# First expert's low weights on VectorE, and shorter slot ranks, at the head of the two capacity-limited expert stages

## The chip, the cores and the metric

One core of one Trainium2 chip. The metric is the device time of one execution in microseconds (us), the median of three runs.

## The reference, cut to what matters

The program is a chain of twelve residual stages on 2048 tokens of 128 features. Stages 0 and 2 are the same mixture of experts, `_L0_ffn_ref`: tokens fall into 8 groups of 256, each token chooses two of 8 experts, and each expert takes at most C = 64 tokens of a group. First choices are counted first, and the rank of a second choice starts behind them.

```python
m1 = one_hot(argmax(softmax(logits)));  m2 = one_hot(argmax(rest))
p1 = cumsum(m1, axis=-2) - m1
m1 = m1 * (p1 < C)
m1_count = sum(m1, axis=-2)
p2 = cumsum(m2, axis=-2) - m2 + m1_count[:, None, :]
m2 = m2 * (p2 < C)
dispatch = (combine != 0)               # one-hot of the slot p1 or p2, per expert
expert_inputs = einsum('GSEC,GSM->EGCM', dispatch, x)
hidden = gelu(expert_inputs @ w0) * (expert_inputs @ w1)
out = einsum('EGCM,GSEC->GSM', hidden @ wo, combine)
```

## The kernel before

Every stage has a program for each engine (TensorE, ScalarE, VectorE, GpSimd, and SyncE, which issues the loads), written out by hand; the engines meet at a barrier before each stage and otherwise by semaphores. `q.wait_ge(*signal.at(key))` is a wait of one engine for a tick of another; on one engine everything behind such a wait stands still. `chain(a)` on VectorE makes each operation wait for the one before it.

`l0_ffn` is the stage concerned; it runs twice, as stage 0 and stage 2. float32 products are made of three passes with float32r operands, `mm3` (lines 94 to 97): high times high, high times low, low times high. So each operand is split into a high part (a cast) and a low part (the difference).

The head of the stage, from the barrier to the first expert product, goes like this.

- SyncE issues the loads of the weights of experts 0, 1 and 2 at once (lines 844 to 847).
- VectorE finds first and second choices (`first_largest`, lines 673 to 680), as masks `m1b` and `m2b`, which TensorE awaits as `mask_set` 1 and 2.
- TensorE makes ranks by products with a triangular matrix `tri` and a matrix of ones `onesb`: first choices into bank 3 (lines 462, 463), the count of first choices per group and expert into bank 4 (465, 466), second choices into bank 5 (468, 469).
- VectorE turns them into slots (lines 688 to 698). A slot is rank plus one, and zero where the token isn't sent. Lines 689 and 696 zero what lies past the capacity, 692 clamps the counts at 64, 694 adds them to the ranks of the second choices.
- VectorE compares slots with 1 to 64 (`iota`), one operation for each of 16 tiles of tokens, 128 x 512 each (line 703): the one-hots `d[t]`.
- TensorE multiplies the features, high and low (z = 0, 1), by the one-hots (line 479, four products for each of 8 groups g), into six banks in turn; ScalarE copies each bank into `xd` (line 610, 16 copies).
- Meanwhile ScalarE has cast the weights of expert 0 (`split_in(0, k)`, line 596), and GpSimd has made their low parts (line 789, k = 0 with 752 columns and k = 1 with 640), ticking `w_lo`.
- The first expert product, `up(0, 0)`, waits for `xd_set` of group 7 and for the low weights (lines 487 to 492). Its first instruction is the one of line 95.

Behind the one-hots VectorE makes the gates `G` (lines 708 to 711), which TensorE needs after `up(0, 1)`, and then it takes part in the experts: `product` (line 717) and `low` (line 722). GpSimd's next work after line 789 is `high(0, 0)` (line 804), behind the first product. The weights of the other seven experts are split by ScalarE and GpSimd within the experts' loop.

```python
for i in range(8):
    high(i, 0)
    high(i, 1)
    if i + 1 < 8:
        split_in(i + 1, 0)
```

Of the kernel before, what the change touches and what calls it, by code (L numbers as in the profile page):

```python
# [7 lines left out]
ALU = mybir.AluOpType  # L8
ACT = mybir.ActivationFunctionType
F32 = mybir.dt.float32  # L10
# [89 lines left out]
def build(nc, ins, out):  # L100
    ctx = ExitStack()
    with ctx:
        signals = []

        def signal(name):
            signals.append(Signal(ctx.enter_context(nc.semaphore(name))))
            return signals[-1]
# [3 lines left out]
        bank = [wide[i // 2][:, i % 2 * 512:i % 2 * 512 + 512] for i in range(8)]  # L111
# [19 lines left out]
        def take(name, n, dt=F32):  # L131
            size = -(-n * (2 if dt == BF16 else 4) // 64) * 64
            a = nc.sbuf_base
            for lo, hi in sorted(mem["used"]):
                if a < hi and a + size > lo:
                    a = hi
            assert a + size <= nc.sbuf_top, (name, n, a + size, nc.sbuf_top)
            mem["n"] += 1
            mem["used"].append((a, a + size))
            return nc.alloc_sbuf_tensor_at(f"{name}{mem['n']}", [128, n], dt, offset=a)[:, :]  # L140
# [17 lines left out]
        def cB(name):  # L158
            a, b = CB_AT[name]
            return cb[:, a:b]  # L160

        ident, iota = cF("ident"), cF("iota")
        identb, tri, onesb = cB("ident"), cB("tri"), cB("ones")
# [10 lines left out]
        step, steppool = signal("dve_step"), signal("pool_step")  # L174
# [6 lines left out]
        w_hi, w_set, w_lo, x_hi, x_set, x_lo = (signal(n) for n in ("w_hi", "w_set", "w_lo", "x_hi", "x_set", "x_lo"))  # L181
        mask_set, rank, slot_set, one_hot, dispatched = (signal(n) for n in ("mask_set", "rank", "slot_set", "one_hot", "dispatched"))
# [233 lines left out]
        def l0_ffn(n, pre, prepare):  # L416
# [4 lines left out]
            w_in = [[twin("w", size) for size in (FH + 64, 640)] for _ in range(3)]  # L421
            wh = [[take("wh", size, F32R) for size in (FH + 64, 640)] for _ in range(2)]
# [4 lines left out]
            passing = mem["used"][first:]  # L427
            ex, tmp, diff, rest, q1, pos = (te3(take(s, 128)) for s in ("ex", "tmp", "diff", "rest", "q1_", "pos"))
            mx, vm = take("mx", 16), take("vm", 16)
            cnt = take("cnt", 64).rearrange("p (g e) -> p g e", e=8)  # L430
            m1b, m2b = take("m1b", 128, BF16), take("m2b", 128, BF16)
            G = take("G", 512).rearrange("p (t n) -> p t n", t=NT)
            gs = take("gs", 32).rearrange("p (g k) -> p g k", k=4)
# [9 lines left out]
            m4 = lambda z: z.rearrange("p (g j e) -> p g j e", j=2, e=8)  # L443
# [14 lines left out]
            def pe(q):  # L458
                e = q.e
# [2 lines left out]
                e.matmul(bank[3][:, 0:128], tri, m1b, start=True, stop=False, skip_group_check=True)  # L462
                e.matmul(m4(bank[3][:, 0:128])[:, :, 1, :], onesb, m4(m1b)[:, :, 0, :], start=False, stop=True,
                         skip_group_check=True).then_inc(*rank.tick(n, 1))
                e.matmul(bank[4][:, 0:64], onesb, m4(m1b)[:, :, 0, :], start=True, stop=False)
                e.matmul(bank[4][:, 0:64], onesb, m4(m1b)[:, :, 1, :], start=False, stop=True).then_inc(*rank.tick(n, "count"))
                q.wait_ge(*mask_set.at(n, 2))
                e.matmul(bank[5][:, 0:128], tri, m2b, start=True, stop=False, skip_group_check=True)
                e.matmul(m4(bank[5][:, 0:128])[:, :, 1, :], onesb, m4(m2b)[:, :, 0, :], start=False, stop=True,
                         skip_group_check=True).then_inc(*rank.tick(n, 2))  # L470
                q.wait_ge(*x_lo.at(n, 3))
# [10 lines left out]
                def up(i, f):  # L482
                    f0, fn = L0T[f]
                    p0, p1 = up_bank(i, f)
                    s = slice(f0, f0 + fn)
                    xe = [xd[:, i, z, :] for z in range(2)]
                    q.wait_ge(*w_hi.at(n, i, 1))
                    q.wait_ge(*w_lo.at(n, i, 1))
                    if 6 * i + f >= 3:
                        q.wait_ge(*mul_set.at(n, *before(i, f)))  # L490
                    else:
                        q.wait_ge(*xd_set.at(n, 7))
                    if f < 5:
                        mm3(e, p0, [wh[i % 2][0][:, s], w_in[i % 3][0][1][:, s]], xe)
                        a = mm3(e, p1, [wh[i % 2][1][:, s], w_in[i % 3][1][1][:, s]], xe)
                    else:
                        a = mm3(e, p0[0:112, :], [wh[i % 2][0][:, 640:752], w_in[i % 3][0][1][:, 640:752]], xe)
                    a.then_inc(*up_done.tick(n, i, f))
# [166 lines left out]
            def dve(q):  # L665
                e = q.e
                t3 = lambda p: p[:, 0:128].rearrange("p (t e) -> p t e", e=8)

                def chain(a):
                    a.then_inc(*step.tick())  # L670
                    q.wait_ge(*step.now())

                def first_largest(v, mask, number, *shifted):
# [9 lines left out]
                m1, m2 = te3(m1b), te3(m2b)  # L683
# [2 lines left out]
                chain(e.scalar_tensor_tensor(rest, m1, 0.5, ex, ALU.is_lt, ALU.mult))  # L686
                first_largest(rest, m2, 2)
                q.wait_ge(*rank.at(n, 1))
                chain(e.scalar_tensor_tensor(tmp, t3(bank[3]), 64.0, m1, ALU.is_lt, ALU.mult))
                chain(e.scalar_tensor_tensor(q1, t3(bank[3]), 1.0, tmp, ALU.add, ALU.mult))  # L690
                q.wait_ge(*rank.at(n, "count"))
                chain(e.tensor_scalar(cnt, bank[4][:, 0:64].rearrange("p (g e) -> p g e", e=8), 64.0, None, ALU.min))
                q.wait_ge(*rank.at(n, 2))
                chain(e.tensor_tensor(rest.rearrange("p (g j) e -> p g j e", j=2), m4(bank[5][:, 0:128]),
                                      cnt.unsqueeze(2).to_broadcast([128, 8, 2, 8]), ALU.add))
                chain(e.scalar_tensor_tensor(tmp, rest, 64.0, m2, ALU.is_lt, ALU.mult))
                chain(e.scalar_tensor_tensor(tmp, rest, 1.0, tmp, ALU.add, ALU.mult))
                e.tensor_tensor(pos, q1, tmp, ALU.add).then_inc(*slot_set.tick(n))

                def one(t):  # L700
                    q.wait_ge(*slot_set.at(n))
                    q.wait_ge(*x_lo.at(n, 3))
                    e.tensor_tensor(d[t].rearrange("p (e c) -> p e c", e=8), iota[:, 1:65].unsqueeze(1).to_broadcast([128, 8, 64]),
                                    pos[:, t, :].unsqueeze(2).to_broadcast([128, 8, 64]), ALU.is_equal).then_inc(*one_hot.tick(n, t))

                for t in range(NT):
                    one(t)
                chain(e.tensor_reduce(mx, ex, X, ALU.add))
                chain(e.reciprocal(mx, mx))
                q.wait_ge(*w_lo.at(n, "pad"))  # L710
# [72 lines left out]
            def pool(q):  # L783
                e = q.e

                def split_in(i, k):
                    w, low = w_in[i % 3][k]
                    q.wait_ge(*w_hi.at(n, i, k))
                    e.tensor_tensor(low, w, wh[i % 2][k].bitcast(F32), ALU.subtract).then_inc(*w_lo.tick(n, i, k))

                def split_out(i):
                    w, low = w_out[i % 2]
                    q.wait_ge(*w_hi.at(n, i, "out"))
                    e.tensor_tensor(low[:, 0:640], w[:, 0:640], woh[i % 2][:, 0:640].bitcast(F32), ALU.subtract)
                    e.tensor_tensor(low[0:48, 640:], w[0:48, 640:], woh[i % 2][0:48, 640:].bitcast(F32),
                                    ALU.subtract).then_inc(*w_lo.tick(n, i, "out"))

                def high(i, f):
                    fn = L0T[f][1]
                    k = 6 * i + f - RING  # L800
                    if k >= 0:
                        q.wait_ge(*down_done.at(n, k // 6))
                    q.wait_ge(*mul_set.at(n, i, f))
                    e.tensor_copy(hid[0][ring(i, f)][0:fn, :], qr[(6 * i + f) % 4][0:fn, :]).then_inc(*hid_hi.tick(n, i, f))

                e.memset(G[:, :, 8:32], 0.0).then_inc(*w_lo.tick(n, "pad"))
                split_in(0, 0)
                split_in(0, 1)
                for i in range(8):
                    high(i, 0)  # L810
                    high(i, 1)
                    if i + 1 < 8:
                        split_in(i + 1, 0)
                    high(i, 2)
                    if i + 1 < 8:
                        split_in(i + 1, 1)
                    split_out(i)
                    high(i, 3)
                    high(i, 4)
                    high(i, 5)  # L820
                for c in range(CHUNKS):
                    finish_pool(q, m, c, nxt)
# [2010 lines left out]
        start = Stage(None, None, None, None, None, {0: 4, 1: 5, 2: 6, 3: 7, "logits": 0}, lambda q, what: None)  # L2833
# [186 lines left out]
```

## Time and profile before

| | us |
|---|---|
| runs | 1792.59, 1788.51, 1789.74 |
| median | 1789.74 |
| profiled execution, its own time | 1807.28 |
| its span, first to last instruction | 1805.5 |
| stage 0: first VectorE operation behind the barrier | 30.83 |
| stage 0: first expert product | 51.36 |
| stage 2: first VectorE operation behind the barrier | 449.85 |
| stage 2: first expert product | 471.00 |

The profile has, besides the page of totals, a timeline (instructions in order of time), tables by line, and busy times in chosen stretches. Starts are counted from the span's first instruction. Where the timeline merges instructions, its second number is the time from the start of the first to the end of the last; instructions of one engine overlap a little, so intervals between starts are shorter than durations.

### The profile page before, as it was taken

How to read it: one execution, taken by the hardware profiler on the slowest of the kernel's cores; microseconds unless marked ns; L12 is line 12 of the kernel's file. 1: busy time of each engine (PE TensorE's matmuls, PEld its weight loads, DVE VectorE, ACT ScalarE, POOL GpSimd, SP SyncE). 2: the span in 40 equal slices, each digit the busy share in tenths (PEclk: the TensorE clock that was granted, in tenths of full speed). 3: DMA queues.
4: the chain of work that ended last, by engine and by line, in shares of the span. 5: the costliest groups of instructions: out<-in, count | busy, mean ns of one | idle time of the engine just before them, and what ended most of it. 6: DMA issues, size and time to landing. Idle time of an engine off the chain costs nothing. (4 is left out here: it accounts for less than half of the span.)

```text
span 1805.5 us, 25127 instructions
## 1 busy us (share of the span) xinstructions
PE 1522.0 (84%) x8766; PEld 1050.0 (58%) x8766; DVE 1221.4 (68%) x2789; ACT 1022.6 (57%) x1826; POOL 625.2 (35%) x764
## 2 busy tenths in 40 slices
PE   4998699997899699849989966996696789996696
PEld 3776333333577588538869955995595322223596
DVE  5787688992788743473335956595686688883685
ACT  2653488885554455345537732773374388885274
POOL 3575311122487100123026724673424211111333
PEclk9999899998899799869989978997798899998698
DMA  3121534300220400010000000000564633300574
GB/s 112 46 74 31 118 42 53 53 1 3 84 75 30 158 1 1 0 47 1 1 1 12 1 1 1 2 1 1 154 193 124 158 62 53 53 1 1 135 204 149
DMA packets 100757, 101.05 MB, mean 56 GB/s; under 512 B 23344, under 2 KB 86360, under 8 KB 99769
## 3 DMA queue, kind: packets, MB, share of 16 engines
q1 hardware_dynamic: 97687, 93.39, 21.4%
q0 software_dynamic: 2944, 6.05, 0.9%
q8 instruction: 70, 1.15, 0.3%
q14 instruction: 56, 0.46, 0.1%
HBM read 87.60 MB, written 15.78 MB: 57 GB/s over the span
## 5 line engine op out<-in xcount | busy, mean ns | idle before, releaser
L2617 DVE TENSOR_REDUCE mx<-bank 128x1 f32<-128x512 f32 (+1 forms) x512 | 320.1, 680 | 56.6 <-PE bank L2408 55.8
L2554 ACT ACTIVATE e<-bank 128x512 f32<-128x512 f32 x512 | 273.1, 600 | 50.4 <-PE bank L2440 47.6
L2440 PE MATMUL bank<-qq,kk 99*128 99x512 bf16 (+1 forms) x512 | 164.2, 386 | 12.9 <-ACT e L2554 12.3
L1546 POOL TENSOR_TENSOR midl<-mid,midh 128x512 fp32r<-128x512 f32 (+1 forms) x96 | 126.1, 1320 | 78.4 <-ACT midh L1466 78.3
L2440 PEld LDWEIGHTS bank<-qq,kk 99*128 99x128 bf16 (+1 forms) x512 | 38.8, 97 | 161.9 <-ACT e L2554 123.1
L1051 DVE TENSOR_TENSOR hl<-q,hh 128x512 fp32r<-128x512 f32 x64 | 44.8, 701 | 125.6 <-ACT hh L1021 103.6
L95 PE MATMUL bank<-wdh,midh 128*128 128x256 f32 (+1 forms) x384 | 113.6, 296 | 9.7 <-DVE x L1530 9.7
L226 POOL TENSOR_SCALAR rs<-mv 128x4 f32<-128x4 f32 x48 | 11.4, 237 | 307.5 <-DVE mv L213 306.6
L97 PE MATMUL bank<-wdh,midl 128*128 128x256 f32 (+1 forms) x384 | 111.1, 289 | 0.0
L96 PE MATMUL bank<-wdl,midh 128*128 128x256 f32 (+1 forms) x384 | 110.9, 289 | 0.0
L2047 POOL DMA_INDIRECT token_y<-y,g x60 | 61.2, 1020 | 134.6 <-DVE y L2016 121.5
L192 PE MATMUL bank<-cf,xn 128*128 128x128 f32 x192 | 41.3, 360 | 74.8 <-DVE xn L245 43.9
L1461 ACT ACTIVATE mid<-bank,bu 128x512 f32<-128x512 f32 (+1 forms) x96 | 65.9, 686 | 64.3 <-PE bank L97 57.1
L97 PE MATMUL bank<-hh,h_l 128*128 128x512 f32 x256 | 99.7, 390 | 0.0
L618 ACT ACTIVATE q<-bank 128x512 f32<-128x512 f32 x96 | 57.2, 596 | 65.8 <-PE bank L97 64.1
L2699 POOL TENSOR_SCALAR mpt<-mx 128x16 bf16<-128x16 f32 (+1 forms) x32 | 11.0, 343 | 238.9 <-DVE mx L2617 238.9
L2408 PE MATMUL bank<-kk,qq 72*128 72x512 bf16 x256 | 80.6, 384 | 11.5 <-DMA kk<-scratch 8.6
L1530 DVE SCALAR_TENSOR_TENSOR x<-ysb,gate,x 128x128 f32<-128x128 f32 x176 | 89.8, 585 | 0.1
L266 ACT COPY xT<-bank 128x512 f32<-128x512 f32 x44 | 25.4, 581 | 111.7 <-PE bank L192 111.7
L2408 PE MATMUL bank<-qq,kk 72*128 72x512 bf16 x256 | 82.5, 387 | 5.7 <-DVE mx L2617 4.1
L717 DVE TENSOR_TENSOR q<-q,bank 128x512 f32<-128x512 f32 x96 | 63.7, 683 | 33.6 <-ACT q L618 32.6
L95 PEld LDWEIGHTS bank<-wdh,midh 128*128 128x128 f32 (+1 forms) x384 | 75.7, 197 | 14.4 <-DVE x L1530 10.1
(406 smaller groups left out, 4514.0 us busy)
## 6 DMA issues: line engine op xcount, KB each, us to landing
w<-in_L_ffn_W SPq DMA_DIRECT2D x30, 512.0 KB
w<-in_L_ffn_W SPq DMA_DIRECT2D x30, 256.0 KB
qq<-scratch SPq DMA_DIRECT2D x18, 384.0 KB
w<-in_L_ffn_w_kernel SPq DMA_DIRECT2D x16, 344.0 KB
w<-in_L_ffn_w_kernel SPq DMA_DIRECT2D x16, 320.0 KB
wo<-in_L_ffn_wo_kernel SPq DMA_DIRECT2D x16, 320.0 KB
scratch<-e SPq DMA_DIRECT2D x34, 128.0 KB, 5.0
sorted<-in_unsorted SPq DMA_DIRECT2D x2, 1935.0 KB, 10.9
```

Of the source, the lines that this page charges most:

```text
L95: e.matmul(o, l[0], r[0], start=start, stop=False)
L96: e.matmul(o, l[0], r[1], start=False, stop=False)
L97: return e.matmul(o, l[1], r[0], start=False, stop=stop)
L717: e.tensor_tensor(v, v, up_bank(i, f)[1] if f < 5 else up_bank(i, f)[0][64:112, :], ALU.mult).then_inc(*mul_set.tick(n, i, f))
L1461: e.activation(z, bank[up_at[i, f] % 3][0:fn, :], ACT.Silu, bias=bu[0:fn, i % 4, f:f + 1]).then_inc(*gelu_set.tick(n, i, f))
L1530: e.scalar_tensor_tensor(x[:, t, :], y[:, h * 128:h * 128 + 128], gate[:, t, 2 * g + h:2 * g + h + 1], x[:, t, :], ALU.mult, ALU.add).then ...
L1546: e.tensor_tensor(l[0:fn, o], mid[i % 2][0:fn, o], h[0:fn, o].bitcast(F32), ALU.subtract).then_inc(*l2_m_lo.tick(n, i, f))
L2047: e.indirect_dma_start(Yd, bass.IndirectOffsetOnAxis(ap=gr[i % RING][:, h, 128:129].bitcast(U32), axis=0), yr[i % RING][:, h, :], None).th ...
L2408: e.matmul(p, l[:, qt * 128:(qt + 1) * 128], r, start=True, stop=True).then_inc(*at_a.tick(n, t, u, j))
L2440: e.matmul(b_bank(t, u, j), keys(kk[0:K], t, b)[:, k * 128:(k + 1) * 128], queries(qq[0:K], t, b), start=True, stop=True).then_inc(*at_b.t ...
L2554: e.activation(er[u][:, j * 512:(j + 1) * 512], b_bank(t, u, j), ACT.Exp, bias=0.0, scale=scale).then_inc(*at_e.tick(n, t, u, j))
L2617: e.tensor_reduce(mxa[t % 3][:, o:o + nkb], bank[place_a["a", t, u, j]].rearrange("p (k n) -> p k n", k=nkb), X, ALU.max).then_inc(*at_max ...
```

## The change

Three edits, all in `l0_ffn`.

- GpSimd no longer makes the low weights of expert 0. VectorE makes them, behind its 16 one-hots and ahead of the gates, and ticks `w_set` in place of `w_lo`; `up(0, f)` waits for that. Experts 1 to 7 stay as they are.
- The slots are made without masks: what lies past slot 64 matches none of the numbers 1 to 64 in the one-hots' comparison. The operations of lines 689, 692, 694 and 696 go, the count's tile too.
- TensorE adds the counts of the first choices to the ranks of the second choices in bank 5, with two products of ones over `m1b` repeated for both tiles of a group, behind the wait for `m2b`. The two products of the counts into bank 4 go.

```diff
-                e.matmul(bank[4][:, 0:64], onesb, m4(m1b)[:, :, 0, :], start=True, stop=False)
-                e.matmul(bank[4][:, 0:64], onesb, m4(m1b)[:, :, 1, :], start=False, stop=True).then_inc(*rank.tick(n, "count"))
                 q.wait_ge(*mask_set.at(n, 2))
-                e.matmul(bank[5][:, 0:128], tri, m2b, start=True, stop=False, skip_group_check=True)
+                for j in range(2):
+                    e.matmul(bank[5][:, 0:128], onesb, m4(m1b)[:, :, j, :].unsqueeze(2).to_broadcast([128, 8, 2, 8]), start=(j == 0),
+                             stop=False, skip_group_check=True)
+                e.matmul(bank[5][:, 0:128], tri, m2b, start=False, stop=False, skip_group_check=True)
...
-                    q.wait_ge(*w_lo.at(n, i, 1))
+                    q.wait_ge(*(w_lo if i > 0 else w_set).at(n, i, 1))
...
                 q.wait_ge(*rank.at(n, 1))
-                chain(e.scalar_tensor_tensor(tmp, t3(bank[3]), 64.0, m1, ALU.is_lt, ALU.mult))
-                chain(e.scalar_tensor_tensor(q1, t3(bank[3]), 1.0, tmp, ALU.add, ALU.mult))
-                q.wait_ge(*rank.at(n, "count"))
-                chain(e.tensor_scalar(cnt, bank[4][:, 0:64].rearrange("p (g e) -> p g e", e=8), 64.0, None, ALU.min))
+                e.scalar_tensor_tensor(q1, t3(bank[3]), 1.0, m1, ALU.add, ALU.mult).then_inc(*step.tick())
                 q.wait_ge(*rank.at(n, 2))
-                chain(e.tensor_tensor(rest.rearrange("p (g j) e -> p g j e", j=2), m4(bank[5][:, 0:128]),
-                                      cnt.unsqueeze(2).to_broadcast([128, 8, 2, 8]), ALU.add))
-                chain(e.scalar_tensor_tensor(tmp, rest, 64.0, m2, ALU.is_lt, ALU.mult))
-                chain(e.scalar_tensor_tensor(tmp, rest, 1.0, tmp, ALU.add, ALU.mult))
+                chain(e.scalar_tensor_tensor(tmp, t3(bank[5]), 1.0, m2, ALU.add, ALU.mult))
                 e.tensor_tensor(pos, q1, tmp, ALU.add).then_inc(*slot_set.tick(n))
...
                 for t in range(NT):
                     one(t)
+                for k in range(2):
+                    w, low_w = w_in[0][k]
+                    q.wait_ge(*w_hi.at(n, 0, k))
+                    e.tensor_tensor(low_w, w, wh[0][k].bitcast(F32), ALU.subtract).then_inc(*w_set.tick(n, 0, k))
...
                 e.memset(G[:, :, 8:32], 0.0).then_inc(*w_lo.tick(n, "pad"))
-                split_in(0, 0)
-                split_in(0, 1)
```

## Rows read from the trace of the kernel before

**Rows 1.** Timeline of stage 0's head: masks, ranks, slots (start, us, engine, line, operation, [idle before]).
```profile
34.40 0.29 DVE L689 SCALAR_TENSOR_TENSOR tmp<-bank,m1b 128x128 f32<-128x128 f32 x1
34.42 0.29 PE L468 MATMUL bank<-m2b,cb 128*128 128x128 bf16 x1 [1.43 <-DVE m2b L679]
34.50 0.26 PE L469 MATMUL bank<-m2b,cb 128*128 128x64 bf16 x1
...
36.17 1.45 ACT L596 CAST wh<-w 128x752 fp32r<-128x752 f32 x2 [4.32 <-DMA w<-in_L_ffn_w_kernel]
36.29 0.29 DVE L698 TENSOR_TENSOR pos<-q,tmp 128x128 f32<-128x128 f32 x1
```

**Rows 2.** Timeline of stage 0: the one-hots and GpSimd's low weights.
```profile
36.61 7.83 DVE L703 TENSOR_TENSOR d<-cf,pos 128x512 fp32r<-128x512 f32 x8
37.07 3.81 POOL L789 TENSOR_TENSOR wl<-w,wh 128x752 fp32r<-128x752 f32 x2 [5.75 <-ACT wh L596]
...
37.22 2.26 DVE L703 TENSOR_TENSOR d<-cf,pos 128x512 fp32r<-128x512 f32 x1
...
41.36 1.28 DVE L703 TENSOR_TENSOR d<-cf,pos 128x512 fp32r<-128x512 f32 x2
...
46.77 2.49 DVE L703 TENSOR_TENSOR xn0r<-cf,pos 128x512 fp32r<-128x512 f32 x4
```

**Rows 3.** Timeline of stage 0: dispatch products, copies into xd, first expert product.
```profile
41.49 1.39 PE L479 MATMUL bank<-d,xn1r 128*128 128x512 f32 x2 [0.30 <-DVE d L703]
45.24 0.94 PE L479 MATMUL bank<-d,xn1r 128*128 128x512 f32 x2
...
46.22 4.99 ACT L610 CAST xd<-bank 128x512 fp32r<-128x512 f32 x10 [0.15 <-PE bank L479]
51.36 0.47 PE L95 MATMUL bank<-xd,wh 128*128 128x512 f32 x1 [1.01 <-ACT xd L610]
```

**Rows 4.** Timeline of stage 2's head, the same places.
```profile
455.58 3.72 POOL L789 TENSOR_TENSOR wl<-w,wh 128x752 fp32r<-128x752 f32 x2 [5.24 <-ACT wh L596]
455.63 2.27 DVE L703 TENSOR_TENSOR d<-cf,pos 128x512 fp32r<-128x512 f32 x1
...
459.90 0.80 PE L479 MATMUL bank<-d,xn1r 128*128 128x512 f32 x1 [1.09 <-DVE d L703]
460.73 0.59 ACT L610 CAST xd<-bank 128x512 fp32r<-128x512 f32 x1 [4.61 <-PE bank L479]
465.85 5.00 ACT L610 CAST xd<-bank 128x512 fp32r<-128x512 f32 x10 [0.27 <-PE bank L479]
471.00 0.47 PE L95 MATMUL bank<-xd,wh 128*128 128x512 f32 x1 [0.99 <-ACT xd L610]
```

**Rows 5.** Stretches: start:end, length, busy PE, PEld, DVE, ACT, POOL; PEclk, DMA share, GB/s.
```profile
39.00:41.00 2.00, 1.46 (x3) 0.83 (x3) 2.00 (x2) 0.59 (x1) 1.88 (x1) 1.00 1.03 360
41.00:43.00 2.00, 1.70 (x4) 1.10 (x4) 2.00 (x4) 0.67 (x2) 0.00 (x0) 1.00 0.09 36
...
60.00:65.00 5.00, 4.83 (x31) 3.87 (x29) 4.24 (x7) 2.79 (x7) 4.03 (x3) 1.00 0.00 0
...
465.00:466.00 1.00, 1.00 (x4) 0.76 (x4) 1.00 (x3) 0.73 (x2) 0.00 (x0) 0.62 0.00 0
```

**Rows 6.** Timeline of stage 0 behind the first products.
```profile
54.32 1.92 PE L530 MATMUL bank<-d,G 128*32 128x512 f32 x16
54.41 0.61 POOL L804 CAST xn1r<-q 128x512 fp32r<-128x512 f32 x1 [13.53 <-DVE q L717]
...
61.94 1.55 POOL L789 TENSOR_TENSOR wl<-w,wh 128x640 fp32r<-128x640 f32 x1
62.01 2.03 DVE L722 TENSOR_TENSOR xT1r<-q,xn1r 128x512 fp32r<-128x512 f32 x1 [0.50 <-POOL xn1r L804]
```

**Rows 7.** Table by line and shape, VectorE: differences of two float32 tiles elsewhere.
```profile
L1998 DVE TENSOR_TENSOR w2l<-w,w2h 128x1024 fp32r<-128x1024 f32 x30 | 36.6, 1221 | 0.9 <-ACT w2h L1911 0.5
L1996 DVE TENSOR_TENSOR w1l<-w,w1h 128x512 fp32r<-128x512 f32 x30 | 20.5, 683 | 0.2
```

More of the change, by code:

```diff
@@ L429, in l0_ffn @@
             mx, vm = take("mx", 16), take("vm", 16)
-            cnt = take("cnt", 64).rearrange("p (g e) -> p g e", e=8)
             m1b, m2b = take("m1b", 128, BF16), take("m2b", 128, BF16)
```

## The prediction

> **What bounds the kernel now.** The page of totals comes first: the profiled execution took 1807.28 us around a span of 1805.5, 17.5 above the median of 1789.74. No engine fills the span, so a local edit is worth what it takes off the chain between the two barriers of a stage. The edit lies in two short stretches, so the view to read is the timeline of each head, from the barrier to the first expert product: 30.83 to 51.36 in stage 0 and 449.85 to 471.00 in stage 2.
>
> First the slots [rows 1]. VectorE goes from one small operation to the next in a little over its 0.29 us, each waiting for the last: pos (line 698) starts at 36.29 and the first one-hot at 36.61, a step of 0.32. TensorE's rank products end long before VectorE uses them: those of the second choices start at 34.42 and 34.50 and end at 34.76.
>
> Then the one-hots [rows 2]. The reader is to see two rates. Undisturbed, two of them take 1.28 us, so one follows another by 0.60. But the first eight take 7.83 where eight at that rate would take 4.88, and the last one-hot ends at 49.26 (46.77 + 2.49). The lost 2.95 us lie where GpSimd makes the low weights, 37.07 to 40.88; a one-hot started at 37.22 lasts 2.26 in place of 0.68. In stage 2, GpSimd starts at 455.58, and there the very first one-hot, at 455.63, takes 2.27 [rows 4]. Both operands of a one-hot, and both of a difference of weights, lie in SBUF.
>
> Then the end [rows 3]. TensorE's products follow each other at a slow pace, two copies 0.85 us apart, until some time in the pair that starts at 45.24, and then twice as fast; ScalarE has ten copies left, runs them without a gap from 46.22 to 51.21, 0.49 apart, and the first expert product starts 0.15 later. So the head ends with ScalarE's backlog, which was built up while TensorE was slow, which started late because VectorE was held. In stage 2 the same: first copy 460.73, seventh 465.85, product 471.00 [rows 4].
>
> **The clock.** In stage 2 the granted clock averages 0.62 from 465 to 466, where TensorE is busy throughout [rows 5]: it rose there from the low level (0.50, 1.2 GHz) to the high one (2.4 GHz), at about 465.8. TensorE had then been busy since 459.90 [rows 4], some 5.9 us. In stage 0 the granted clock is shown as 1.00 throughout, but the products have the slow pace of the low level until 45.24 or a little later [rows 3, 5]; I go by the pace. There the gapless work began at 41.49, some 4.1 us before. The Trainium skill, "TensorE: Matmul & The Clock Gate", section "Seeing it yourself", warns that these clock records can be unreliable; stage 0 agrees.
>
> **Slots.** Gone from VectorE's chain are lines 689, 692, 694 and 696. Line 690's successor starts where 689 did, at 34.40, and must then wait for the ranks. TensorE's two new products (128 columns) stand between the wait for m2b and the old pair. The old pair starts 0.08 apart; at the low pace (two products of 512 columns start 0.43 apart) 128 columns take 0.11, so the two add 0.16 to 0.22. I take the larger, since the clock is low: ranks at 34.76 + 0.21 = 34.97. The two products of counts that go lay off the path. With 0.05 for the semaphore, what is left of line 697 starts at 35.02, where before it started a step ahead of pos, at 35.96: 0.94 us saved in each stage. Bounds: 1.16 if the products cost nothing (then 34.80), 0.57 if they overlap nothing and take the 0.29 of line 468 each. The first one-hot then starts at S = 36.61 - 0.94 = 35.67 in stage 0, and 454.69 in stage 2.
>
> **One-hots.** GpSimd has nothing left to do between its memset and 54.41 [rows 6], so all sixteen run at 0.60: the last ends at S + 15 x 0.60 + 0.68 = S + 9.68, which is 45.35, against 49.26.
>
> **TensorE and ScalarE.** The structure is that of stage 2 before: the first product alone, then from the second one-hot on work without a gap, since at the low clock TensorE needs 0.85 for what VectorE brings in 0.60. First copy: second one-hot ends at S + 1.28, product 0.63 at the low pace and 0.07 for the two starts: S + 1.98 = 37.65. ScalarE's casts of the weights end at 37.62 (36.17 + 1.45) [rows 1], so they just don't hold it. With n copies 0.85 apart while the clock is low and the other intervals of 0.49, the last copy ends at S + 1.98 + 0.85 n + 0.49 (15 - n) + 0.59 = S + 9.92 + 0.36 n. Checked on stage 2 before: 460.73 - 1.98 + 9.92 + 0.36 x 6 = 470.83, and the copies end at 470.85. The two spells, of 5.9 and 4.1 us, give n = 6 and n = 4; I take 5: S + 11.72. The floor, if the clock rises so early that VectorE bounds: last one-hot, two products at the fast pace (0.86 to the end of the second), a copy 0.63: S + 11.2.
>
> **VectorE's new work.** Differences of this kind take 683 ns for 512 columns and 1221 for 1024 [rows 7], 1.05 ns per column: 0.94 for 752 and 0.82 for 640. Behind the last one-hot they end at S + 9.60 + 0.94 + 0.82 - 0.07 = S + 11.3, 0.4 before ScalarE is done. So they cost nothing at n = 5; without that cover (n = 3 or less) they cost 0.1. They would decide alone only if both together took over 2.1 us, and eat up the gain only beyond 6.0. The gates move with them, to S + 12.3 = 48.0; their products came 2.96 behind the first expert product [rows 6], so now at about 50.5: covered. product(0, 0) needs VectorE later still.
>
> **Sum.** The first expert product starts 0.15 behind the last copy: 35.67 + 11.87 = 47.54 against 51.36, a gain of 3.8; in stage 2, 454.69 + 11.87 = 466.56 against 471.00, 4.4. Behind it nothing I see is tied to a fixed time: the loads issued at the barrier, of experts 0 to 2, are through at about 41 (DMA share 1.03 from 39 to 41, 0.09 from 41 to 43) [rows 5], so expert 1 is there before 47, and later loads wait for products. So 8.2 us: 1789.7 - 8.2 = 1781.5.
>
> **Rivals.** (1) *The one-hots were held by the loads, not by GpSimd.* For it: the 16 DMA engines are full while they are slow, share 1.03 at 360 GB/s from 39 to 41, 0.09 behind it [rows 5], and the last slow one-hot ends at about 41.4 [rows 2]. Against: in stage 2 the first one-hot is slow as soon as GpSimd works, in stage 0 not yet; and at 62.01 a VectorE difference takes 2.03 beside GpSimd's line 789 in a stretch with DMA share 0.00 [rows 5, 6]. Then only the slots' 0.9 and a trifle are gained per stage, 1787.8. The skill's page "SBUF — State Buffer" says that DMA doesn't contend with an engine there, and that VectorE and GpSimd take their shared ports by an exclusive lock held for the whole instruction; the trace agrees, as far as 62.01 shows it. It also covers the case that the change doesn't do what it says. Chance 0.05.
>
> (2) *The clock falls again.* Once fast, TensorE has 0.93 us of work for each 1.20 that VectorE takes per group, so its gapless run ends, where before it had a backlog to the end. If the clock falls and a low spell of 4.1 to 5.9 us lies on the first expert's products (0.43 in place of 0.23 each), each costs 0.46 of its length, 2.3 us: gain 8.2 - 4.6, so 1786.1. Chance 0.06.
>
> (3) *Slower: the clock doesn't rise in the dispatch at all.* n = 15 gives S + 15.3, which is 51.1: the head's gain is gone but for 0.2, and the low spell then lies on the experts, 2.3 us or more in each stage: 1794. It decides if the low spell lasts from the first copy past all sixteen, 12.8 us; both spells seen are under half. The page on TensorE, Part 1, says that the default state is throttled and that activity releases it; that activity is no thinner here while the clock is low. Chance 0.03.
>
> **How the numbers follow.** The forecast has 0.86. Its own range: largest savings of the slots and the floor in both stages, 4.6 + 5.1 = 9.7, so 1780.0; n = 8 and the smallest, 2.4 + 3.0 = 5.4, so 1784.3. Add the 2 us by which runs of this kernel lie about their median: 1778 to 1786.5, which also takes in half of rival 2. Measurement can tell about 0.2% (3.6 us) from no change, so faster is below 1786.2. Faster 0.85, same 0.12, slower 0.03.
>
> **What the changed profile should show.** One-hots with no duration above 0.7, the first at about 35.7 and 454.7, the last ending near 45.4 and 464.4; line 789's GpSimd rows 30 and not 32; two VectorE differences of 0.94 and 0.82 behind them; copies 0.85 apart and then 0.49; the first expert product at 47.5 and 466.6, less whatever stage 1 shifts. I am wrong if one-hots are slow without GpSimd, if granted clock 0.50 lasts into the experts, or if stage 0 ends earlier by much less than its first product starts earlier.

## The result, and the profile after

The changed kernel takes 1782.73 us (median of ten runs, 1781.12 to 1786.23), the kernel before 1791.51 (ten runs, 1788.51 to 1797.88). The ratio is 0.995, 95% interval 0.9939 to 0.9961: 9.0 us faster, 7.0 to 10.9. The forecast was 8.2 us and 1781.5, in a range of 1778.0 to 1786.5.

The profiled execution took 1781.12 us around a span of 1779.2. Its span can't be set against the 1805.5 of before: that execution lay 17.5 us above its kernel's median of the first three runs, and the excess lies behind stage 2. From stage 2's first addition to x to the end of the span there are 1210.1 us in before, against 1191.4 in the changed kernel and 1192.5 in e2 (below), all with the same instructions there. What can be compared is the length of the two heads, each from its own barrier.

This is the timeline of stage 0 in the changed kernel, in the columns of [rows 1]; it answers to [rows 1 to 3].

```profile
30.20 0.28 DVE L674 TENSOR_REDUCE mx<-lg 128x16 f32<-128x128 f32 x1 [5.98 <-POOLq L349]
...
33.77 0.29 DVE L689 SCALAR_TENSOR_TENSOR q<-bank,m1b 128x128 f32<-128x128 f32 x1
33.79 0.40 PE L466 MATMUL bank<-m1b,cb 128*128 128x128 bf16 x2 [1.54 <-DVE m2b L679]
33.98 0.31 PE L468 MATMUL bank<-m2b,cb 128*128 128x128 bf16 x1
34.09 0.26 PE L469 MATMUL bank<-m2b,cb 128*128 128x64 bf16 x1
34.38 0.29 DVE L691 SCALAR_TENSOR_TENSOR tmp<-bank,m2b 128x128 f32<-128x128 f32 x1 [0.32 <-PE bank L469]
34.71 0.29 DVE L692 TENSOR_TENSOR pos<-q,tmp 128x128 f32<-128x128 f32 x1
35.04 4.91 DVE L697 TENSOR_TENSOR d<-cf,pos 128x512 fp32r<-128x512 f32 x8
...
37.22 0.59 ACT L610 CAST xd<-bank 128x512 fp32r<-128x512 f32 x1
...
40.53 5.97 ACT L610 CAST xd<-bank 128x512 fp32r<-128x512 f32 x12 [0.17 <-PE bank L479]
...
44.67 1.67 DVE L705 TENSOR_TENSOR wl<-w,wh 128x752 fp32r<-128x752 f32 x2
...
46.65 0.47 PE L95 MATMUL bank<-xd,wh 128*128 128x512 f32 x1 [0.87 <-ACT xd L610]
```

The reader is to see four things. The operation on the second choices' ranks now waits 0.32 us for TensorE, as it should, and the first one-hot starts 4.84 us behind the barrier, where before it was 36.61 - 30.83 = 5.78: 0.94 less. Eight one-hots take 4.91 us, where before they took 7.83 [rows 2]. VectorE's two differences start when the one-hots end and are done at 46.34. ScalarE's last twelve copies run without a gap to 46.50, and the first expert product follows 0.15 later. The head is 16.45 us long against 20.53.

Stage 2, the same view, answers to [rows 4].

```profile
446.56 0.29 DVE L674 TENSOR_REDUCE mx<-lg 128x16 f32<-128x128 f32 x1 [6.77 <-POOLq L349]
...
453.56 0.59 ACT L610 CAST xd<-bank 128x512 fp32r<-128x512 f32 x1 [0.52 <-PE bank L479]
...
456.92 5.97 ACT L610 CAST xd<-bank 128x512 fp32r<-128x512 f32 x12 [0.21 <-PE bank L479]
...
461.02 1.67 DVE L705 TENSOR_TENSOR wl<-w,wh 128x752 fp32r<-128x752 f32 x2
...
463.04 0.47 PE L95 MATMUL bank<-xd,wh 128*128 128x512 f32 x1 [0.92 <-ACT xd L610]
```

16.48 against 21.15. The two heads together save 4.08 + 4.67 = 8.75 us, which lies inside the interval of the measured 9.0 (7.0 to 10.9). The kernel before was profiled once, and its heads too depend on how many copies are slow, so the sum of the heads is good to about half a microsecond in each stage (by e11 below).

The stretches of stage 2 in the changed kernel, in the columns of [rows 5]:

```profile
455.00:456.00 1.00, 1.00 (x4) 0.77 (x3) 1.00 (x3) 0.59 (x2) 0.00 (x0) 0.50 1.07 385
456.00:457.00 1.00, 1.00 (x5) 0.78 (x4) 1.00 (x3) 0.67 (x2) 0.00 (x0) 0.66 0.60 230
457.00:458.00 1.00, 1.00 (x6) 0.82 (x5) 1.00 (x2) 1.00 (x3) 0.00 (x0) 1.00 0.12 29
```

From 455 to 456 the DMA engines are full (share 1.07) while one-hots go at their undisturbed pace (all sixteen of this stage take 0.68 or 0.69 us): the rival that blamed the loads has lost its ground already here. And the granted clock rises from 0.50 to 1.00 in the microsecond that averages 0.66, so at about 456.7. TensorE had then been busy without a gap since its first dispatch product at 452.22, for 4.5 us.

### The profile page after: what moved, and what is told of

It reads as the page before. It is cut to its first block and busy times, and to the rows that moved or that the text cites. A ratio compares the mean times of both kernels' runs of the same rounds, so it can differ in the third digit from the quotient of the medians.

```text
span 1779.2 us, 25115 instructions
## 1 busy us (share of the span) xinstructions
PE 1514.6 (85%) x8766; PEld 1043.1 (59%) x8766; DVE 1217.0 (68%) x2785; ACT 1021.4 (57%) x1826; POOL 625.2 (35%) x760
## 5 line engine op out<-in xcount | busy, mean ns | idle before, releaser
L1542 POOL TENSOR_TENSOR midl<-mid,midh 128x512 fp32r<-128x512 f32 (+1 forms) x96 | 131.6, 1380 | 73.4 <-ACT midh L1462 73.3
```

The lines of the kernel that those rows point to most:

```text
L1542: e.tensor_tensor(l[0:fn, o], mid[i % 2][0:fn, o], h[0:fn, o].bitcast(F32), ALU.subtract).then_inc(*l2_m_lo.tick(n, i, f))
```

## The experiments

The head is measured in each from the first VectorE operation behind the barrier to the first expert product, stage 0 / stage 2. Ratios are to the kernel before on the same chip.

| run | head, us | saved, sum | ratio, 95% interval |
|---|---|---|---|
| before | 20.53 / 21.15 | | |
| after | 16.45 / 16.48 | 8.75 | 0.9950 (0.9939 to 0.9961) |
| e1 low weights alone | 17.30 / 18.17 | 6.21 | 0.9957 (0.9941 to 0.9973) |
| e2 short slots alone | 19.53 / 20.34 | 1.81 | 0.9982 (0.9973 to 0.9991) |
| e3 GpSimd reads | 20.47 / 20.23 | 0.98 | 0.9993 (0.9982 to 1.0003) |
| e4 GpSimd fills | 16.82 / 16.95 | 7.91 | 0.9957 (0.9943 to 0.9972) |
| e5 before, slots in PSUM | 17.23 / 17.25 | 7.20 | 0.9976 (0.9959 to 0.9992) |
| e6 short slots in PSUM | 16.29 / 16.29 | 9.10 | 0.9950 (0.9931 to 0.9969) |
| e7 differences twice | 17.82 / 17.83 | 6.03 | 0.9977 (0.9961 to 0.9992) |
| e8 TensorE kept busy | 16.35 / 16.35 | 8.98 | 0.9949 (0.9932 to 0.9967) |
| e9 differences in the middle | 17.95 / 17.95 | 5.78 | 0.9975 (0.9965 to 0.9986) |
| e10 e6 and e8 together | 16.19 / 16.11 | 9.38 | 0.9956 (0.9943 to 0.9969) |
| e11 after again | 16.92 / 16.36 | 8.40 | 0.9948 (0.9935 to 0.9960) |

An interval is 3 to 7 us wide, so the ratios order these kernels roughly, and the heads say what happened. e1 to e4 ran on one chip, where the kernel before took 1792.73 us, e5 to e8 on a second (1790.66) and e9 to e11 on a third (1808.87). What the third takes more lies behind stage 2 (1210.7 us from its first addition to x to the end in e11, 1191.4 in after); the ratios and heads of the kernel after are nearly the same there. Heads are of one profile each, before's of the one shown ahead of the prediction; the two profiles of the kernel after (after and e11) differ by 0.47 in stage 0 and 0.12 in stage 2.

**The two parts alone.** e1 is the kernel before with the low weights of expert 0 moved, e2 the one with the short slots and the low weights on GpSimd.

```diff
                 for t in range(NT):
                     one(t)
+                for k in range(2):
+                    w, low_w = w_in[0][k]
+                    q.wait_ge(*w_hi.at(n, 0, k))
+                    e.tensor_tensor(low_w, w, wh[0][k].bitcast(F32), ALU.subtract).then_inc(*w_set.tick(n, 0, k))
...
-                split_in(0, 0)
-                split_in(0, 1)
```

This is e1, on the kernel before, with the wait of `up` changed as in the kernel after. e2 is the kernel after with these lines, and that wait, the other way round.

> The kernel before with only the low weights of expert 0 moved to VectorE behind the one-hots; the slots are made as before. My theory (GpSimd's two differences hold VectorE's one-hots): one-hots 0.60 apart without a slow one, first expert product 3.1 us (4.08 less the slots' 0.94) nearer to the barrier in stage 0, 3.7 in stage 2, so about 6.9 us faster than before (1784.6 against 1791.5). Rival (the loads hold the one-hots): one-hots as slow as before, product at most 0.3 us nearer, time within 1 us of before.

> The kernel before with only the short slots; GpSimd makes the low weights of expert 0 as before. My theory: the first one-hot is 0.94 us nearer to the barrier, two one-hots are still slow (2.0 to 2.3 us each), the first expert product is 0.6 to 0.95 nearer in each stage: 1.2 to 1.9 us faster than before. Rival (the two edits need each other: with the lock in place TensorE's restart is set by GpSimd's end, which follows the landing of the weights): the product moves by under 0.3 us, time within 0.6 us of before.

e1: one-hots 0.60 apart in both stages, heads 3.23 and 2.98 us shorter, ratio 0.9957, so 7.7 us (4.8 to 10.6). In stage 2 the gain is below what was expected, 3.7: six copies were slow there, where after has four. e2: the first one-hot is nearer by 0.95 us, two one-hots are still slow (2.03 to 2.31 us), heads 1.00 and 0.81 shorter where at most 0.95 was expected, ratio 0.9982, 3.2 us (1.6 to 4.8). The parts' heads add up to 8.02 against 8.75 for both. The rival that they need each other falls.

**What holds the one-hots.** e3 and e4 are the kernel after with useless work for GpSimd at the old place, once with reads of SBUF, once without. It writes into a tile `junk`, added for it.

```diff
                 e.memset(G[:, :, 8:32], 0.0).then_inc(*w_lo.tick(n, "pad"))
+                for k, size in enumerate((752, 640)):
+                    q.wait_ge(*w_hi.at(n, 0, k))
+                    e.tensor_tensor(junk[:, 1392 - size:1392] if size == 640 else junk[:, 0:752], cf[:, 0:size], cf[:, 752:752 + size], ALU.subtract)
```

That is e3, and e4 has in its place:

```diff
                 e.memset(G[:, :, 8:32], 0.0).then_inc(*w_lo.tick(n, "pad"))
+                q.wait_ge(*w_hi.at(n, 0, 0))
+                for k in range(5):
+                    e.memset(junk[:, 0:752], 0.0).then_inc(*steppool.tick())
+                    q.wait_ge(*steppool.now())
```

> The kernel after, and GpSimd does two differences of the old sizes again (752 and 640 columns, constants in SBUF as operands, result never used) where it made the low weights. Nothing else is changed. My theory (lock): VectorE's one-hots beside them are slow again, two of about 2.0 to 2.3 us, the last one ends some 2.9 us later, the first expert product 3 us or more later in each stage: 6 to 7.5 us slower than the kernel after. Rival (loads): no one-hot is slow, time as after, within 0.5 us.

> The kernel after, and GpSimd fills a tile five times with zero (752 columns each, 0.8 to 0.9 us each) where it made the low weights: as long as the two differences, but without a read of SBUF. If it is the read of SBUF by GpSimd that holds an operation of VectorE with two operands in SBUF: one-hots stay 0.60 apart, time as after within 0.5 us. Rival (any GpSimd operation in SBUF holds VectorE): one-hots beside the fills last over 1 us, time 3 us or more above after.

The timeline of e3, stage 0:

```profile
35.35 7.88 DVE L698 TENSOR_TENSOR d<-cf,pos 128x512 fp32r<-128x512 f32 x8
...
36.71 4.17 POOL L808 TENSOR_TENSOR junk<-cf 128x752 f32<-128x752 f32 x2 [5.69 <-ACT wh L597]
...
51.00 0.47 PE L95 MATMUL bank<-xd,wh 128*128 128x512 f32 x1 [0.89 <-ACT xd L611]
```

The same view of e4:

```profile
35.34 4.90 DVE L698 TENSOR_TENSOR d<-cf,pos 128x512 fp32r<-128x512 f32 x8
...
37.31 3.86 POOL L808 MEMSET junk<- 128x752 f32 x5 [6.31 <-ACT wh L597]
...
47.33 0.47 PE L95 MATMUL bank<-xd,wh 128*128 128x512 f32 x1 [1.04 <-ACT xd L611]
```

GpSimd's work lasts 4.17 us in one and 3.86 in the other, at nearly the same time, beside the same loads. With reads, eight one-hots take 7.88 us; without, 4.90. e3 gives the low weights' gain back: its heads are 7.77 us longer than after's (6 to 7.5 was expected), and its ratio is that of no change. So it is not GpSimd's work as such, nor its writes, nor the loads: it is GpSimd's reads of SBUF. Taken one by one, the operations of e3 show turns: GpSimd's first difference runs from 36.71 to 38.92, and the one-hot that starts at 37.16 ends at 39.46; the second difference, from 38.87, ends at 40.87, and the next one-hot, from 39.39, at 41.42. Each ends 0.54 to 0.55 us behind GpSimd's, a little less than the 0.68 that a one-hot takes alone.

e4's fills differ from e3's differences in kind too, but the experts of the kernel after show that a GpSimd operation with a single operand in SBUF is enough. In its timeline (the first two rows, and two from a little later):

```profile
61.66 0.60 POOL L802 CAST hid<-q 128x512 fp32r<-128x512 f32 x1
61.74 1.07 DVE L720 TENSOR_TENSOR xT1r<-q,xn1r 128x512 fp32r<-128x512 f32 x1 [0.80 <-POOL xn1r L802]
...
67.28 2.24 POOL L787 TENSOR_TENSOR wl<-w,wh 128x752 fp32r<-128x752 f32 x1
...
67.78 0.68 DVE L715 TENSOR_TENSOR q<-q,bank 128x512 f32<-128x512 f32 x1
```

Beside a cast, which reads one tile, a VectorE difference of two tiles in SBUF takes 1.07 us in place of 0.68. VectorE's product of 67.78, with one operand in PSUM, takes 0.68 beside a GpSimd difference.

e4's heads are 0.37 and 0.47 longer than after's; five copies were slow there, not four, worth 0.36 each by the prediction's own formula (in stage 0 ScalarE's casts of the weights also held the first copy, until 37.79).

e5 takes away the other side: the kernel before, GpSimd's differences and all, but the one-hots read the slots from PSUM, so only one of VectorE's operands is in SBUF. The edit is the same on the kernel before:

```diff
+                slots_p = t3(bank[7])
...
-                e.tensor_tensor(pos, q1, tmp, ALU.add).then_inc(*slot_set.tick(n))
+                e.tensor_tensor(slots_p, q1, tmp, ALU.add).then_inc(*slot_set.tick(n))
...
-                                    pos[:, t, :].unsqueeze(2).to_broadcast([128, 8, 64]), ALU.is_equal).then_inc(*one_hot.tick(n, t))
+                                    slots_p[:, t, :].unsqueeze(2).to_broadcast([128, 8, 64]), ALU.is_equal).then_inc(*one_hot.tick(n, t))
```

> The kernel before, whole, but VectorE writes the slots (pos) into bank 7 of PSUM and the one-hots read them there; GpSimd still makes the low weights of expert 0. My theory (the lock needs two operands of VectorE in SBUF): no slow one-hot though GpSimd works beside them; the head as in the run with the low weights alone moved, 3 to 3.7 us shorter per stage, 1784 to 1786. Rival (GpSimd's read of SBUF holds VectorE whatever VectorE reads): two slow one-hots, time as before. A third: reading slots from PSUM makes each one-hot slower (0.05 us or more), which takes 0.8 us per stage off the gain.

The timeline of e5, stage 0:

```profile
36.16 3.30 POOL L790 TENSOR_TENSOR wl<-w,wh 128x752 fp32r<-128x752 f32 x2 [5.25 <-ACT wh L596]
36.20 4.87 DVE L704 TENSOR_TENSOR d<-cf,bank 128x512 fp32r<-128x512 f32 x8
...
47.65 0.47 PE L95 MATMUL bank<-xd,wh 128*128 128x512 f32 x1 [0.79 <-ACT xd L610]
```

Both engines start within 0.04 us of each other and neither holds the other: eight one-hots in 4.87, and GpSimd's two differences in 3.30, where beside the old one-hots they took 3.81 [rows 2]. No operation moved to another engine, and the heads are 3.30 and 3.90 us shorter. The time is less clear than the heads: 0.9976, so 4.3 us, with an upper end of 7.3 that just takes in the heads' 7.2; the median of 1787.76 lies above the 1784 to 1786 expected. The Trainium skill, "SBUF — State Buffer", section "SBUF: two separate sides", says that on the port pair that the two engines share a VectorE operation with two SBUF inputs contends only with a GpSimd operation that reads SBUF, by an exclusive lock. The runs agree with each of the three conditions: two inputs in SBUF (e3 against e5), a read by GpSimd (e3 against e4), and turns (e3's operations one by one).

**How much cover is left.** e7 doubles VectorE's differences, e9 puts them behind the eighth one-hot.

```diff
                 for t in range(NT):
                     one(t)
+                for size in (752, 640):
+                    e.tensor_tensor(junk[:, 1392 - size:1392] if size == 640 else junk[:, 0:752], cf[:, 0:size], cf[:, 752:752 + size], ALU.subtract)
                 for k in range(2):
                     w, low_w = w_in[0][k]
```

That is e7. In e9 the loop over `k` stands inside the loop over `t`:

```diff
                 for t in range(NT):
                     one(t)
-                for k in range(2):
-                    w, low_w = w_in[0][k]
+                    if t == 7:
+                        for k in range(2):
+                            w, low_w = w_in[0][k]
...
```

> The kernel after, and VectorE does two more differences of the same sizes (752 and 640 columns, constants, result unused) between the one-hots and the two that make the low weights. My theory (the cover is all but used up, 0.16 us left): 1.75 us more work, so the first expert product 1.4 to 1.6 us later in each stage, 2.8 to 3.2 us above after. Rival (still covered by ScalarE's copies or by what comes behind, the gates and the table load): under 1 us above after.

> The kernel after, with VectorE's two differences in the middle of the one-hots (behind the eighth) and not behind the last. My theory: one-hots 8 to 15 come 1.6 us later, VectorE then is what the last copy waits for (last one-hot at S + 9.68 + 1.6, then 1.5 to the end of the copies): first expert product 1.3 to 1.5 us later than in after in each stage, 2.6 to 3.0 us slower. Rival (ScalarE's backlog hides it): product within 0.3 us of after, time within 0.6 us.

The timeline of e7, stage 0:

```profile
44.69 1.67 DVE L704 TENSOR_TENSOR junk<-cf 128x752 f32<-128x752 f32 x2
46.27 1.67 DVE L708 TENSOR_TENSOR wl<-w,wh 128x752 fp32r<-128x752 f32 x2
46.45 1.28 ACT L619 ACT_TABLE_LOAD   x1
48.04 0.47 PE L95 MATMUL bank<-xd,wh 128*128 128x512 f32 x1 [2.26 <-DVE wl L708]
```

For the first time the product waits for VectorE's differences: they end at 47.94, the last copy had ended by 46.45, where ScalarE's table load starts. 1.58 us of extra work cost 1.37 and 1.35 (1.4 to 1.6 was expected), so 0.2 was covered and no more. In e9 the copies are what it waits for, but they wait for one-hots that come 1.58 later: 1.50 and 1.47 lost. The place behind the last one-hot is worth nearly what the differences last, and it holds them with 0.2 us to spare.

**The clock.** e8 keeps TensorE busy with products of constants in the gaps of the routing.

```diff
+                keep_warm(q, bank[7], 4)
                 q.wait_ge(*mask_set.at(n, 1))
...
+                keep_warm(q, bank[7], 4)
                 q.wait_ge(*mask_set.at(n, 2))
...
+                keep_warm(q, bank[7], 4)
                 q.wait_ge(*x_lo.at(n, 3))
```

> The kernel after, and TensorE multiplies constants (three times four products of 416 columns into bank 7, unused) in the gaps of the routing: behind the barrier, before the wait for the second choices, and behind the ranks. It computes nothing of the output. My theory of ScalarE's backlog: the clock is high when the one-hots come, n falls from 4 to 0 or 1, and the head ends at the floor set by VectorE, 11.2 to 11.3 us behind the first one-hot plus 0.15, where after has 11.6: first expert product 0.15 to 0.3 us earlier in each stage, time 0 to 0.6 us below after. Rival (the low clock costs more than that, as products of the experts are also held): more than 1 us faster. If the added products delay the ranks, the first one-hot comes later by up to 0.4 us.

The timeline of e8, stage 0:

```profile
37.18 9.50 ACT L613 CAST xd<-bank 128x512 fp32r<-128x512 f32 x16 [0.21 <-PE bank L482]
...
44.94 1.67 DVE L708 TENSOR_TENSOR wl<-w,wh 128x752 fp32r<-128x752 f32 x2
46.82 0.47 PE L95 MATMUL bank<-xd,wh 128*128 128x512 f32 x1 [0.78 <-ACT xd L613]
```

And the stretches of its stage 2:

```profile
450.00:452.00 2.00, 1.94 (x8) 0.80 (x8) 1.61 (x5) 0.25 (x1) 0.00 (x0) 0.50 1.02 317
452.00:454.00 2.00, 1.86 (x6) 1.05 (x7) 2.00 (x4) 2.00 (x4) 0.00 (x0) 0.98 0.94 309
```

The granted clock is 0.98 from 452 to 454, where the dispatch begins, no copy is slow, all sixteen take 9.50 us at VectorE's pace of two per 1.2. Both heads come to 16.35: the floor, 0.10 and 0.13 below after, where 0.15 to 0.3 was expected. In stage 0 of the kernel before, the last copy ended 1.95 us behind the last one-hot [rows 2, 3]; in after it is 1.74, here 1.66. So little is left of what the slow clock costs. Nearly the same, 1.66 or 1.67, stands in e7 and e6 in both stages and in e11's stage 2, though up to three copies are slow there: with so few, VectorE's pace decides when the last copy ends, and ScalarE's backlog no longer does.

**A version that takes all of it.** e6 is the short slots, in PSUM, with the low weights left on GpSimd; its edit on the kernel after is e5's and the one below, and `up` waits for `w_lo` again. e10 adds e8's products to that, in bank 6.

```diff
-                for k in range(2):
-                    w, low_w = w_in[0][k]
-                    q.wait_ge(*w_hi.at(n, 0, k))
-                    e.tensor_tensor(low_w, w, wh[0][k].bitcast(F32), ALU.subtract).then_inc(*w_set.tick(n, 0, k))
...
+                split_in(0, 0)
+                split_in(0, 1)
```

> The short slots of the kernel after, slots in bank 7 of PSUM, and the low weights of expert 0 still on GpSimd: a candidate that takes both gains without giving VectorE the differences. My theory: head as in the kernel after, since there the differences end just ahead of the last copy (46.34 against 46.50): first expert product 16.4 to 16.9 us behind the barrier, time within 0.1% of after. If VectorE's differences cost something later in the stage, it is faster than after by that.

> The three together: short slots in PSUM, low weights of expert 0 on GpSimd beside the one-hots, TensorE kept busy in the routing (products of constants, unused). Nothing but the sixteen one-hots is left between the slots and the end: first expert product at 4.83 + 9.65 + 1.5 + 0.15, 16.1 to 16.3 us behind the barrier in both stages, against 16.45 and 16.48 in after; time 0.3 to 0.7 us below after, which the runs can't tell from no change. If it is more than 2 us faster, something behind the head was held by VectorE's differences or by the clock.

> The kernel after itself, beside the two others on one chip: ratio to before 0.994 to 0.996, and the head as in its first profile but for the number n of slow copies (4 in both stages there, 2 to 6 expected), which moves the first expert product by 0.36 us for each, within 16.4 to 17.2.

e6 has the shortest heads without useless products, 16.29 in both stages (16.4 to 16.9 was expected), at a ratio of 0.9950: as fast as after, and VectorE has two operations less in each stage. e10's are 16.19 and 16.11, its first one-hots starting 4.73 and 4.65 behind the barrier in place of 4.83; its ratio is 0.9956 beside 0.9948 for after on the same chip. Nothing here beats the changed kernel by what the runs can tell; the heads end at VectorE's sixteen one-hots in e6, e8 and e10. e11 repeats after: TensorE's products were slow for five copies in stage 0 and for three in stage 2, heads 16.92 and 16.36, the second just below the 16.4 to 17.2 expected. In stage 0 ScalarE's casts also held the first copy until 7.73 us behind the barrier, the weights having landed late.

## Why the prediction was right, point by point

- **Slots.** The step of 0.94 us was measured at 0.94. The two added products took 0.19 to the start of the old pair (33.79 to 33.98), the estimate was 0.21.
- **One-hots.** 0.60 apart, the first at S = 35.04, the last ends at 44.76, 9.72 behind it; 9.68 was forecast. That GpSimd's reads hold the one-hots was argued before from four rows; e3, e4 and e5 show it, and with it that both operands of the one-hot must lie in SBUF, which the prediction noted without a run that tests it.
- **Copies.** The formula S + 9.92 + 0.36 n gives 46.40 for n = 4; they ended at 46.50. The term that was off is n: I took 5, the mean of the two spells, and it was 4 in both stages. That is 0.36 us in each, and with the 0.1 of the formula the head came out at 16.45 and 16.48 where 16.71 was forecast (47.54 - 30.83). In e1 alone it was 2 in stage 0 and 6 in stage 2, so a forecast of it to one is luck. Two parts of this sum were off without showing. The first copy came at S + 2.18, not S + 1.98, in both stages. And the floor was taken as S + 11.2, where e8 shows S + 11.38 in both stages. For n = 3 the formula gives S + 11.00, below that floor, and e7 and e11's stage 2, with three slow copies, ended at S + 11.38 or 11.39. After ended only 0.09 and 0.13 above the floor, so one slow copy less would have gained it a tenth, not 0.36.
- **Differences.** 0.94 + 0.82 was forecast, less 0.07: 1.69. Measured 1.67 from first start to last end. They ended 0.16 us before the copies, in place of 0.4. e7 shows that cover to be 0.2 us.
- **The sum.** 3.8 + 4.4 forecast, 4.08 + 4.67 in the trace, 9.0 by the runs (7.0 to 10.9).
- **Behind the head.** From the first expert product to the first addition to x takes 124.3 or 124.8 us, in either stage, and either value occurs in variants of both kernels (stage 0: 124.3 or 124.4 before, in e3 and in e9, 124.8 in the others; stage 2: 124.3 or 124.4 before, in e5, e10 and e11, 124.8 in the others). Only e7's stage 2 is longer, 125.9. The profile of before has the short value twice and that of after the long one twice, 0.85 us together, but e11, the same kernel as after, has the short one in stage 2. So the change doesn't fix the value, and no run shows that it gives anything back in the experts; what makes the half microsecond was not tried.
- **The rivals.** The loads: excluded by after's own stretches and by e3 and e4. The clock falling again, or not rising: it rose during the dispatch in every profile (in e8 and e10 before it), and the first expert product took 0.47 us, the fast form. e8 bounds what it could still matter at 0.13.

The granted clock shown in stage 0 can't be used: in e3 it is 1.00 from 37 to 43 us, beside copies 0.85 apart (37.53 and 38.38). The pace of the products was the better witness there.

## What to carry to other kernels

Before moving work between VectorE and GpSimd, look at what each reads: an elementwise operation of VectorE with two operands in SBUF and a GpSimd operation that reads SBUF run one behind the other, and here that cost 2.9 us of one-hots for 3.8 us of side work. Two cures are shown: move the side work behind the last operation that matters (after), or put one of VectorE's operands into PSUM (e5, no work moved). GpSimd work that doesn't read SBUF needs none (e4). And when a queue is let free, ask what bounds next: before, ScalarE's backlog held the last copy 0.29 and 0.92 us past the 1.66 behind the last one-hot that VectorE's pace allows; after, it is about 0.1, VectorE's one-hots set the head, and the cover behind which the moved work lies is 0.2 us thick.

## What the runs showed that I had not expected

- With the slots in PSUM a one-hot is no slower than with both operands in SBUF: eight take 4.87 us against 4.91.
- GpSimd loses too: its two differences take 3.72 to 4.17 us beside one-hots with two SBUF operands (before, e2, e3), 3.30 to 3.38 beside one-hots that read PSUM (e5, e6, e10).
- In e2 and e3 the slow one-hots cut TensorE's run in two, and the second part began slowly once more: in e2, stage 2, copies come at 460.27, 461.12, 461.98, 462.83 and 463.68 us, 0.85 apart, after a gap of 3.3 us. There the last copy ends 2.67 us behind the last one-hot, against 1.79 in after. So such a hold costs its own length and a slow start behind it.
